# An audio tower on one core: the joined product ahead of the keys, the first tap on ScalarE, attention factors in halves, and products that nobody reads

## The reference

```python
# front: depthwise convolution (7 taps) and pointwise product, relu, maximum of pairs
h = conv(x, w_dw, K=7, groups=192) + b_dw
h = relu(einsum('od,bds->bos', w_pw, h) + b_pw)
h = max_pool_of_2(h)                              # 375 tokens
h = layernorm(real(fft2(h))) * gamma + beta
# token attention, 12 heads of 64
w = heads(layernorm(h) @ w_qkv)
Pi = softmax(sum((w / norm(w))**2, -1) * temp)     # norm and softmax over the tokens
dots = einsum('bhn,bhnd->bhd', Pi / sum(Pi), w * w)
h = h + (-(w * Pi) * 1 / (1 + dots)) @ w_out + b_out
# middle: routed attention on layernorm(h), 12 heads of 16
normed = ln(layernorm(h), g1, b1)
scores = sigmoid(normed @ Wr + br)
chosen = the 56 tokens with the lowest scores
attn_out = softmax(q k^T / 4) v @ Wo + bo         # used in the chosen tokens
mix_out = (normed + scores * pooled) @ Wm + bm    # used in all others
h2 = layernorm(h) + where(chosen, attn_out, mix_out)
# last: gelu(ln(h2) @ W1 + bf1) @ W2 + bf2, added to h2 and to h
```

## Time and profile before

| | us |
|---|---|
| median of three runs (593.9 to 599.0) | 594.25 |
| the profiled execution | 593.38 |
| its span | 591.6 |
| TensorE busy | 492.6 (83% of the span) |
| VectorE busy | 437.3 (74%) |
| ScalarE busy | 233.2 (39%) |
| GpSimd busy | 68.4 (12%) |

### The profile page before, as it was taken

How to read it: one execution, slowest core, us unless ns; L and a number is a source line. 1 busy time by engine, 2 the same in 40 slices (tenths; PEclk the granted TensorE clock), 3 DMA queues, 4 the chain that set the end, 5 groups by cost and what they waited for, 6 DMA issues and landing times.

```text
span 591.6 us, 8840 instructions
## 1 busy us (share of the span) xinstructions
PE 492.6 (83%) x2992; PEld 409.7 (69%) x2992; DVE 437.3 (74%) x1256; ACT 233.2 (39%) x611; POOL 68.4 (12%) x67
## 2 busy tenths in 40 slices
PE   1637497969989998989889988999899979867786
PEld 1425376649777787778876876797778867756676
DVE  6778669786987897888888888788788485853340
ACT  0134113542447135722483256424571358113621
POOL 0010001101120003001210112011200040001000
PEclk9987599798989998999999999999899999978889
DMA  8430100010001000010001000100000000000001
GB/s 241 127 115 1 39 1 2 0 40 2 0 1 41 7 14 2 7 34 19 0 0 39 19 0 0 39 19 0 0 0 9 12 1 0 2 21 0 2 6 34
DMA packets 8392, 13.26 MB, mean 22 GB/s; under 512 B 1911, under 2 KB 6834, under 8 KB 8365
## 3 DMA queue, kind: packets, MB, share of 16 engines
q1 hardware_dynamic: 8365, 12.92, 7.8%
HBM read 10.61 MB, written 2.30 MB: 22 GB/s over the span
## 4 chain that ended last, share of the span: by engine, by line
PE 58%; DVE 22%; ACT 8%; issue 7%; POOL 2%; DMA 1%; ACTq 0%; DVEq 0%; SPq 0%; POOLq 0%
PE xb L1211 9%; PE zb L1109 8%; PE xb L1153 6%; PE yb L1372 4%; POOL rs L828 2%; DVE dw L409 2%; PE zb L1320 2%; DVE junk L530 2%; PE xb L1192 2%; DVE w_sq L522 2%; PE xb L1116 2%; PE xb L1143 2%; ACT w_sq L915 2%; PE zb L1101 2%; PE xb L1144 2%
## 5 line engine op out<-in xcount | busy, mean ns | idle before, releaser
L391 DVE SCALAR_TENSOR_TENSOR dw<-x_in,w_dw_sb,dw 96x750 f32<-96x750 f32 x84 | 78.7, 991 | 0.4
L828 POOL TENSOR_TENSOR rs<-ve,half 125x3 f32<-125x3 f32 (+1 forms) x32 | 33.5, 1046 | 384.2 <-DVE ve L374 310.0
L1211 PE MATMUL xb<-scratch,w_sq 128*125 128x192 f32 x288 | 52.5, 344 | 10.7 <-ACT scratch L926 10.7
L1211 PEld LDWEIGHTS xb<-scratch,w_sq 128*125 128x125 f32 x288 | 50.4, 200 | 13.0 <-DVE scratch L544 13.0
L1372 PE MATMUL yb<-w_sb,gelu 128*125 128x192 f32 x252 | 48.1, 334 | 0.0
L1372 PEld LDWEIGHTS yb<-w_sb,gelu 128*125 128x125 f32 x252 | 42.6, 193 | 1.2 <-issue 1.2
L1116 PE MATMUL yb<-n2T,w_sb 128*128 128x376 f32 x48 | 21.6, 450 | 17.4 <-ACT gelu L1009 13.5
L1153 PE MATMUL xb<-dft_n_sb,pooled_h 125*96 125x376 f32 x96 | 34.0, 506 | 1.0 <-DVE pooled_h L425 0.9
L522 DVE TENSOR_TENSOR w_sq<-w_s,xb 128x376 f32<-128x376 f32 x48 | 25.2, 538 | 9.5 <-PE xb L1203 9.5
L1009 ACT ACTIVATE gelu<-yb,b_sb 128x375 f32<-128x375 f32 x48 | 26.7, 571 | 12.6 <-PE yb L1124 11.7
L1003 ACT ACTIVATE n2T<-zb 128x375 fp32r<-128x375 f32 (+1 forms) x16 | 7.7, 481 | 60.5 <-PE zb L1101 60.3
(11 more groups left out here) (204 smaller groups left out, 1226.3 us busy)
## 6 DMA issues: line engine op xcount, KB each, us to landing
x_in<-in_x SPq DMA_DIRECT2D x8, 567.0 KB, 4.2
out<-res_f SPq DMA_DIRECT2D x7, 281.2 KB
gelu<-in_w_qkv SPq DMA_DIRECT2D x1, 768.0 KB, 6.5
gelu<-in_w SPq DMA_DIRECT2D x1, 768.0 KB, 4.3
w_out_sb<-in_w_out SPq DMA_DIRECT2D x1, 576.0 KB
w_sb<-in_w SPq DMA_DIRECT2D x1, 576.0 KB
rows_sb<-in_rows SPq DMA_DIRECT2D x1, 504.0 KB
dft_n_sb<-in_dft_n SPq DMA_DIRECT2D x1, 493.5 KB
```

Source lines behind the costliest of these rows:

```text
L391: ins = dve.scalar_tensor_tensor(out=dw[0:C, c, :], in0=src, scalar=w_dw[:, c, k:k + 1], in1=dw[0:C, c, :], op0=ALU.mult, op1=ALU.add)
L828: pool.tensor_tensor(out_[:], in_[:], half3[:] if len(in_.shape) == 3 else half3[:, 0, :], ALU.pow).then_inc(rs.sem, 1)
L1211: ins = mm(o, u[:, j, tok(t)], w_oa[:, j, :], start=(j == 0), stop=(j == IT - 1))
```

## The change

On TensorE the joined product goes ahead of the keys (`values_keys`); its third piece goes to bank xb[:, 1] and so waits until ScalarE has read the transform over tokens. `score_sums` follows the keys at once, then `over_channels` (with two added waits, for the banks' readers), then the forward pieces 1 and 2, then `ranks`. The front's input is transposed into xb[:, 1], no longer into zb[:, 2]. Here is TensorE in the loop, behind the transform over tokens; zb, xb and yb are the banks, before:

```diff
+        def joined(t):
+
+            return zb[0:P, t] if t < 2 else xb[0:P, 1]
...
-            return zb[:, 2] if c == 0 else yb[:, 1]
+            return xb[:, 1] if c == 0 else yb[:, 1]
...
+            def attention_factors(b, h):
+
+                part = slice(3 * h, 3 * h + 3)
+                dve.wait_ge(*dots_done.of(b, 3 * h + 3))
+                dve.tensor_tensor(natt[:, part], dots[:, part], u[:, part, N], ALU.mult).then_inc(att_steps.sem, 1)
+                dve.wait_ge(*att_steps.of(b, 3 * h + 1))
+                dve.tensor_scalar(natt[:, part], natt[:, part], -1.0, -1.0, ALU.mult, ALU.add).then_inc(att_steps.sem, 1)
+                dve.wait_ge(*att_steps.of(b, 3 * h + 2))
+                dve.reciprocal(natt[:, part], natt[:, part]).then_inc(att_steps.sem, 1)
+
             def scaled_weights(b):
...
+                dve.wait_ge(*att_steps.of(b))
...
-                taps = ((0, 4), (4, 5), (5, 6), (6, 7), (7, 7), (7, 7))
+                taps = ((1, 4), (4, 5), (5, 6), (6, 7))
...
                     spectrum_norm(p)
+                if front:
+                    second_norm(p)
+                if middle:
+                    queries(q)
+                if front:
+                    front_input(p)
                 if middle:
                     unselected_scores(q)
-                if front:
-                    second_norm(p)
-                if middle:
-                    queries(q)
-                if front:
-                    front_input(p)
...
                     attention_out(q)
                 if front:
+                    attention_factors(p, 0)
                     token_products(p, 5, 6)
+                    attention_factors(p, 1)
                     scaled_weights(p)
-                depthwise(w, *taps[4])
...
-                    pool.wait_ge(*sb_ready.of(q))
+                    pool.wait_ge(*sc_steps.of(q))
...
+            def first_tap(b):
+                if b is None:
+                    return
+                act.wait_ge(taps_in.sem, 16)
+                act.wait_ge(*x_ready.of(b))
+                act.wait_ge(*pw_ready.before(b))
+                for c in range(CT):
+                    act.activation(dw[0:C, c, :], x_in[:, c, 0:S], ACT.Identity, scale=w_dw[:, c, 0:1], bias=w_dw[:, c, K:K + 1])\
+                       .then_inc(dw_first.sem, 1)
...
-                act.wait_ge(*att_steps.of(b))
+                act.wait_ge(*att_steps.of(b, 3))
...
+            def values_keys(b):
+                for k, (t0, t1) in enumerate(((0, 2), (2, 3))):
+                    act.wait_ge(*v_ready.of(b, k + 1))
+                    src = zb[0:P, 0:2, D] if k == 0 else joined(2)[:, D:D + 1]
+                    act.activation(sexp[:, t0:t1], src, ACT.Exp, scale=-1.0).then_inc(sexp_done.sem, 1)
+                if not first(b):
+                    act.wait_ge(*pv_ready.before(b))
                     act.wait_ge(*ql_ready.before(b))
+                for k, (t0, t1) in enumerate(((0, 2), (2, 3))):
+                    src = zb[0:P, 0:2, 0:D] if k == 0 else joined(2)[:, 0:D].unsqueeze(1)
+                    act.activation(v[:, t0:t1, :], src, ACT.Copy).then_inc(v_done.sem, 1)
                 for c in range(CT):
                     act.wait_ge(*k_ready.of(b, c + 1))
-                    act.activation(kT[:, c, 0:N], zb[0:C, 2 + c, 0:N], ACT.Identity, bias=b_k[:, c:c + 1]).then_inc(kT_done.sem, 1)
...
+                    act.activation(kT[:, c, 0:N], zb[0:C, 3 - c, 0:N], ACT.Identity, bias=b_k[:, c:c + 1]).then_inc(kT_done.sem, 1)
...
+                first_tap(w)
                 if front:
                     spectrum_parts(p)
                 if middle:
-                    keys_values(q)
+                    values_keys(q)
...
-                if middle:
-                    copy_scores(q)
                 if last:
                     gelus(r, 0)
                     gelus(r, 1)
+                if middle:
+                    copy_scores(q)
+                if last:
                     gelus(r, 2)
...
                     turned(q, 0)
-                    turned(q, 1)
                     token_exp(p)
-                    for j in range(2, IT):
+                    for j in range(1, IT):
                         turned(q, j)
...
+            def over_channels(b, q):
 
                 pe.wait_ge(*fcs_done.of(b))
+                if q is not None:
+                    pe.wait_ge(*v_done.of(q))
+                    pe.wait_ge(*zm_done.of(q))
...
-                if q is not None:
-                    pe.wait_ge(*sc_row_done.of(q))
...
-                pe.wait_ge(*woa_done.of(b))
                 pe.wait_ge(*woa_act_done.of(b))
                 for t in range(T):
                     o = xb[0:P, t // 2, D * (t % 2):D * (t % 2) + D]
                     for j in range(IT):
+                        if t == 0 and j == 3:
+                            pe.wait_ge(*woa_done.of(b))
                         ins = mm(o, u[:, j, tok(t)], w_oa[:, j, :], start=(j == 0), stop=(j == IT - 1))
...
+                for t in range(T):
+                    if t == 2 and p is not None:
+                        pe.wait_ge(*fcs_done.of(p))
+                    o = joined(t)[:, 0:DV + D]
                     split_product(o, nT[:, :, 0, tok(t)], w_vm[:, :, 0, :], True, False)
                     ins = split_product(o, nT[0:C, :, 1, tok(t)], w_vm[0:C, :, 1, :], False, True)
                     if t:
                         ins.then_inc(v_ready.sem, 1)
+                for k in range(CT):
+                    for c in range(CT):
+                        ins = split_product(zb[0:C, 3 - k, 0:NE], w_k[:, :, c, chan(k)], nT[0:C, :, c, :], c == 0, c == 1)
+                    ins.then_inc(k_ready.sem, 1)
...
-                pe.wait_ge(*kT_done.of(b))
+                pe.wait_ge(*kT_done.of(b, 1))
                 pe.wait_ge(*sc_steps.of(b, 2))
                 for t in range(T):
                     ins = pe.transpose(zb[0:P, 3, tok(t)], nr[:, t, 1, C:C + 1].to_broadcast([P, P]), ident[0:P, 0:P])
                 ins.then_inc(sb_ready.sem, 1)
 
             def ranks(b):
+                pe.wait_ge(*kT_done.of(b))
+                pe.wait_ge(*less_done.of(b))
+                for t in range(T):
+                    ins = mm(zb[0:Q + 1, 2, 0:N], ones_bf[:], less[:, t, 0:N], start=(t == 0), stop=(t == T - 1))
+                ins.then_inc(rk_ready.sem, 1)
+
+            def slots(b):
                 pe.wait_ge(*v_done.of(b))
                 pe.wait_ge(*zm_done.of(b))
...
+            def idle_products(bank, n):
+
+                for _ in range(n):
+                    mm(bank[0:P, 0:2 * KF], dft_n[:, 0, 0:P], dft_n[:, 0, :], start=True, stop=True)
+
...
+                alone, second, drain = front and not middle, front and middle and not last, middle and not front
...
+                if drain:
+                    pe.wait_ge(*h1_done.of(q))
+                    idle_products(xb[:, 0], 3)
...
+                    values_keys(q, p)
+                if middle:
+                    score_sums(q)
+                if front:
+                    over_channels(p, q)
+                if alone:
+                    idle_products(zb[:, 0], 11)
                 if last:
                     forward_up(r, 1)
-                if middle:
-                    score_sums(q)
-                if front:
-                    over_channels(p)
-                if last:
                     forward_up(r, 2)
+                if second:
+                    idle_products(yb[:, 0], 2)
                 if middle:
                     ranks(q)
                 if last:
                     forward_up(r, 3)
+                if second:
+                    idle_products(yb[:, 0], 1)
                 if middle:
                     slots(q)
...
-                    front_input(p, q, r)
+                    front_input(p, r)
...
+                if alone:
+                    idle_products(zb[:, 0], 2)
+                if second:
+                    pe.wait_ge(*prob_done.of(q, 3))
+                    idle_products(yb[:, 0], 2)
...
+                if alone:
+                    idle_products(zb[:, 0], 4)
...
+                if second:
+                    idle_products(yb[:, 0], 1)
...
                     values(q, 0)
+                if front:
+                    spread(p, 2)
+                if middle:
+                    values(q, 1)
+                if front:
+                    spread(p, 3)
+                if alone or second:
+                    idle_products(zb[:, 0] if alone else yb[:, 0], 1)
                 if last and front:
                     for j in range(3, IT):
                         forward_down(r, 1, j)
...
+                if alone:
+                    idle_products(zb[:, 0], 4)
+                if second:
+                    idle_products(yb[:, 0], 3)
```

More of the change, by code:

```diff
@@ L1454, in step @@
                     values(q, 0)
-                if last and front:
-                    for j in range(3, IT):
```

(1 more changed line is left out.)

83 lines of the change are left out of this document (32 added, 51 removed).

## The result

The changed kernel takes 566.5 us (median of four runs, 563.3 to 572.7) against 596.6 for the kernel before on the same chip: ratio 0.948, 95% interval 0.939 to 0.957 (the ratio leaves out the run of 572.7, which is over 1.5% above the fastest). Its profiled execution took 564.93, with a span of 563.1 and a mean granted clock of 0.97 (before: 593.38, 591.6, 0.935).

What follows compares the result with a forecast made beforehand. TensorE's queue was taken to set the time, through its waits and lower clock. Gains of 17.1 + 3.5 + 5.0 + 1.5 + 4.0 = 31.1 from 593.38 gave 562.3; with 0.87 for the median, 563 us, range 552 to 576.

Steps and rivals of the forecast that it cites:

- head of a step: Loop step up to the front's transposes: earlier scores, statistics and ranks save 1.6 us, bounds 1.16 to 2.0.
- tail of a step: Token output at the loop step's end: its wait for all six factors goes, saving 1.25 us, bounds 0.75 to 1.4.
- six steps without low stretches: Loop steps 2 to 7: head and tail gains of 2.85 us a step, together 17.1, bounds 11.5 to 20.4.
- low stretches in steps 2 to 7: Short lower-clock stretches in steps 2, 3 and 6: a shorter gap before saves half, 1.5 us, bounds 0 to 3.
- step 0: 22 idle products in its gaps hold the clock, surest at the token output: 3.5 us saved, bounds 1.55 to 7.05.
- step 1: The loop step's 2.85 plus the clock held by 12 idle products: 5.0 us saved, bounds 2.85 to 9.9.
- steps 8 and 9: Forecast for step 8: earlier rank product and clock gain, less three idle products on the path: 4.0 us, bounds -1 to 6.7.
- the 60.6 that was to show the forecast wrong: Loop steps staying over 60.6 us would mean only the head or the tail gained; 59.4 was forecast.
- So this circle is open: Ranks, score row and gelus in a loop step: TensorE's 1.56 wait and VectorE's 0.64 wait were to go.
- The rival of the tail given back: End of a loop step: VectorE's slack is used up, only the head's 1.6 counts, 573 us; chance 0.2.
- The rival that they don't: Steps 0, 1 and 8: idle products do not hold the clock, only the order gains, 574 us; chance 0.1.
- The one that they are the path: Idle products run at the lower clock, 49.6 us, with 39 uncovered by gaps, 612 us; chance 0.03.

Runs made afterwards that it cites:

- e10: Changed kernel with the keys ahead of the joined product again, on TensorE and ScalarE: 582.8 us, ratio 0.977.
- e6: Changed kernel with the row of unselected scores ahead of the front's second norm again: 564.9 us, ratio 0.941.
- e7: Changed kernel with POOL (GpSimd) waiting for the score sums again before its residuals: 565.1 us, ratio 0.942.
- e8: Changed kernel with the old order of gelu and score row: ranks between forward pieces 1 and 2, score row ahead of gelus 0 and 1: 561.2 us, ratio 0.935.
- e5: Changed kernel with the six attention factors computed together again behind the last token product: 568.2 us, ratio 0.944.
- e9: Changed kernel with the first tap on VectorE again and none on ScalarE: 565.6 us, ratio 0.946.
- e1: Changed kernel without any of the 37 products that nobody reads, nor the waits ahead of those of steps 1 and 8: 566.2 us, ratio 0.946.
- e4: Kernel before, in its own order, with only the 34 idle products of steps 0 and 1 added: 594.25 us against 599.6, ratio 0.991.
- e2: Changed kernel without the three idle products of step 8 and their wait: 562.1 us, ratio 0.940.
- e3: Changed kernel with two more idle products in each of steps 2 to 7, ahead of the front's transposes: 562.2 us, ratio 0.938.
- e11: Changed kernel with the old order of gelu and score row in steps 2 to 7 only, and no products in step 8: 556.5 us, ratio 0.931.
- e12: As e11, but with five idle products in step 8 ahead of forward piece 0: 553.5 us, ratio 0.928.

## Why the prediction was right, and where it was off

The forecast was 563, the time is 566.5: 30.1 less than the kernel before, where 31.2 were forecast. By its terms, in the profiled executions:

| term | predicted | measured |
|---|---|---|
| head of a step | 1.6 | 1.80 |
| tail of a step | 1.25 | 1.15 |
| six steps without low stretches | 17.1 | 17.7 (6 x 2.95) |
| low stretches in steps 2 to 7 | 1.5 | -1.7 (15.97 in all, less 17.7) |
| step 0 | 3.5 | 3.37 |
| step 1 | 5.0 | 4.45 |
| steps 8 and 9 | 4.0 | 4.66 |
| sum | 31.1 | 28.5 with 0.05 at the start |

Of the signs named beforehand, a loop step without a low stretch (59.28 for 59.4), the waits of 1.56 and 0.75 that went, ScalarE's pair and the 1.44 in step 8 came as said. The gap ahead of the front's transposes did not, and by the low stretches behind it steps 3, 4 and 6 take 60.7 to 60.9, over the 60.6 that was to show the forecast wrong; that bound had left the clock out.

Two more rows of VectorE in the kernel before bear on the head: the first comparison, and what follows `unselected_scores`.

```profile
348.66 0.85 DVE L608 SCALAR_TENSOR_TENSOR less<-zb,nr,later_sb 125x125 bf16<-125x125 f32 x3
...
359.98 0.96 DVE L469 TENSOR_SCALAR even<-res,ag,rs 125x192 f32<-125x192 f32 x3 [0.39 <-POOL rs L828]
```

- **The head's size was right, several of its pieces were not, so that its nearness is in part luck.** The joined product ahead is the core (e10: 1.5 a step). "It then runs through with no wait" was wrong: the scores came 2.0 earlier and then VectorE waited 0.95 for the score sums. "`unselected_scores` is certainly off this path" was wrong as a gain: the row had stood in VectorE's wait for POOL all the time, and the earlier trace rows showed only the row, not the wait behind it (e6: 0). The wait for POOL counted 0.42 and is worth 0.2 (e7), because behind it the rank product ended last. "So this circle is open" was right of the wait, but the forward piece ahead of the ranks costs 0.37 (e8): the earlier scores alone had undone the wait. The comparisons started 0.95 earlier and not 0.7 (16.17 into the step, then 15.22), which made up for it: with the 0.42 and the fall of the rank wait from 0.64 to 0.29 that is 1.72 of the 1.80. (0.7 + 0.42 is 1.12, not 1.16; the range does not hang on it.)
- **The tail** went as said: the halves give 0.69 (e5) of 1.15; the rest lies between the front's transposes and the token output. That the 0.75 was only in ScalarE's path, and VectorE had slack, holds: its last wait fell from 1.11 to nothing and 0.13 was given back (token output to next step 6.57, then 6.70). The rival of the tail given back is out: a step gained 2.95 and not 1.6. It was right that VectorE's slack would be used up.
- **ScalarE's pair** took 1.91, not 1.6; the idle time behind it, 1.32, covers that. By the Trainium skill, "ScalarE: Activation LUTs", section "What ACT_TABLE_LOAD costs", it was 1.9: the trace agrees. The copy of the earlier trace rows that I priced it by has no operands per partition. On VectorE the tap would cost 0.45 a step (e9, step 2) and not 1.24, since VectorE waits for the score sums at that place.
- **The products** hold the clock, as the terms of steps 0 and 1 say, at 0.65 each (22 passes in 7.14). The rival that they don't is out by e1 and e4 (3.25 and 2.30; 1.9 and 4.5), though step 1's share is not clear of the scatter in the new order. The one that they are the path holds in step 8 alone: there they took 3.83 at the lower level, and the joined product came 3.0 later than in e2. The forecast's price of 2 to 4 was right; that the clock behind pays for it is not shown (low stretches of 10 in both traces). They did not stand "behind a wait of their own" either: TensorE ran straight into them.
- **The short stretches** are the term with the wrong sign. I expected half of them to go with the gap of 1.56. It went, but the gap of 1.52 ahead of the front's transposes, which I had said would be 1.2 to 1.4, takes its place: four stretches, 1.4 to 1.6 each. Filled (e3) or cut to 0.74 (e8, e11, e12) it brings none in 24 steps. The Trainium skill, "TensorE: Matmul & The Clock Gate", Part 1, says that the count of slow products differs from run to run; the traces agree, though from two kernels: the same instructions of steps 2 to 7 took 376.3 and, in e4, 387.0.

## What to carry to other kernels

Before you count an edit as "off the path", look at what the engine does behind it: a row that stands in a wait for another engine costs nothing, and moving it gives nothing. When one edit makes a result earlier, try the edits made for the same wait one by one without the others; here one of them had turned into a loss. Filler work pays in a gap that another engine ends; behind the gap, where TensorE had work ready, the same products stood on the path.

## What the runs showed of the hardware

In the changed kernel and six of its variants (e1, e2, e5, e6, e7, e9) TensorE stands 1.5 us ahead of the front's transposes in steps 2 to 7, and the granted clock fell to the lower level just behind that gap in 3 to 5 of the six steps of each trace, for some 3.4 us (6.8 in e5); in the changed kernel such a step is 1.4 to 1.6 longer. With the gap at 0.74 or less (e3, e8, e11, e12) it fell in none of 24 steps. How much of the lower clock one piece of code meets differs between traces: steps 2 to 7 of the kernel before had 10 us of it, and the same instructions in e4, behind 34 added products in steps 0 and 1, had 38 and steps of 64.9 where the shortest had been 62.2. Whether the products did that or the execution is not shown.
